# A graph network kernel on one core: order of waits in the packed attention stage, lag of twelve steps, eighteen staged chunks

## The reference, cut to what matters

```python
h = relu(layernorm(x))
x_l = h @ W_l + b_l;  x_r = h @ W_r + b_r           # 4 heads of 32
m = leaky_relu(x_l[s] + x_r[d], 0.2)                # s, d: edges and self loops
e = einsum('ehc,hc->eh', m, att)
alpha = exp(e - segment_max(e)[d]) / segment_sum(...)[d]
x = x + segment_sum(alpha * x_l[s], d) + bias
h = relu(layernorm(x))
msg = (h @ W_in2f)[src] * (ssp(f_ij @ Wf1 + bf1) @ Wf2 + bf2) * rcut
x = x + ssp(segment_sum(msg, dst) @ Wo1 + bo1) @ Wo2 + bo2
```

## Time and profile before

| what | value |
|---|---|
| median of 3 runs | 3136.14 us (3135.15 to 3142.57) |
| the profiled execution, its own time | 3137.6 us |
| its span, first to last instruction | 3135.7 us |
| mean granted clock of TensorE | 0.916 |
| busy: PE, DVE, ACT, POOL | 78%, 72%, 61%, 60% of the span |
| stage D, about 0 to 475 us | DMA engines 89% busy |
| stage A, about 475 to 1555 us | DMA engines 49% busy |
| stage B, about 1555 to 2760 us | DMA engines 61% busy |
| stage F, about 2760 to 3136 us | DMA engines 94% busy |

### The profile page before, as it was taken

One profiled execution on the slowest core, in us unless ns is written; L12 is line 12 of the kernel. 1 busy time (PEld: TensorE's weight loads), 2 busy tenths in 40 slices (PEclk: granted clock), 3 DMA queues, 4 the chain that ended last, 5 costly groups with the idle time before them and its releaser, 6 DMA issues.

```text
span 3135.7 us, 59629 instructions
## 1 busy us (share of the span) xinstructions
PE 2438.1 (78%) x16506; PEld 1688.5 (54%) x16506; DVE 2269.0 (72%) x6293; ACT 1924.9 (61%) x4383; POOL 1884.0 (60%) x1646
## 2 busy tenths in 40 slices
PE   5988897887888888888677777776777777578887
PEld 4666663344444444444455555555555555467776
DVE  6777775676777777676587777777877777557666
ACT  5888886555555555554165555555555555378887
POOL 2677774366766666672168888888878888700000
PEclk8999999999999899898598999999988988889999
DMA  7999983355545555554355666666566565589998
GB/s 215 296 322 315 288 275 127 119 168 154 163 153 168 171 178 180 149 170 139 108 117 111 120 117 113 118 114 121 113 117 115 116 121 110 136 311 424 426 426 334
DMA packets 389182, 590.96 MB, mean 188 GB/s; under 512 B 148024, under 2 KB 225196, under 8 KB 363923
## 3 DMA queue, kind: packets, MB, share of 16 engines
q1 hardware_dynamic: 291106, 478.16, 46.6%
q0 software_dynamic: 97968, 111.60, 18.7%
HBM read 352.81 MB, written 245.42 MB: 191 GB/s over the span
## 4 chain that ended last, share of the span: by engine, by line
DMA 22%; DVE 22%; issue 16%; POOL 12%; PE 12%; ACT 10%; SPq 6%; DVEq 0%; POOLq 0%; ACTq 0%
POOL sum_dram L737 7%; DMA out<-d_x 7%; DMA d_x<-in_x 4%; POOL x_dram L725 4%; DMA b_end<-ends 3%; ACT a_ns L1296 3%; DMA sum_dram<-b_sum,b_at 2%; DVE stat_e_six L958 2%; DVE a_o L1076 2%; PE bank L1530 2%; DVE a_pv L1070 2%; DVE a_gate L1068 2%; DVE stat_e_six L960 2%; DMA x_dram<-b_xo,sidx 2%; DVE stat_d_six L882 2%
## 5 line engine op out<-in xcount | busy, mean ns | idle before, releaser
L737 POOL DMA_INDIRECT sum_dram<-b_sum,b_at x392 | 636.8, 1624 | 146.7 <-issue 112.8
L651 POOL DMA_INDIRECT a_xs<-in_x,index x328 | 334.4, 1020 | 112.0 <-issue 103.7
L658 POOL DMA_INDIRECT a_xd<-in_x,index x328 | 333.0, 1015 | 100.0 <-issue 94.2
L725 POOL DMA_INDIRECT x_dram<-b_xo,sidx x294 | 314.7, 1070 | 105.9 <-issue 91.6
L1669 PE MATMUL bank<-b_rows,b_same 128*128 128x128 bf16 x4704 | 303.6, 229 | 0.6 <-ACT b_sum L1437 0.6
L1669 PEld LDWEIGHTS bank<-b_rows,b_same 128*128 128x128 bf16 x4704 | 288.7, 103 | 0.6 <-issue 0.6
L1277 ACT ACTIVATE d_n<-d_x,stat_d_shift,stat_d_rstd 128x128 f32<-128x128 f32 x686 | 283.5, 486 | 0.2 <-DVE stat_d_shift L773 0.2
L667 POOL DMA_INDIRECT x_dram<-a_xo,index x98 | 101.0, 1030 | 298.8 <-DVE a_xo L1091 280.2
L1702 PE MATMUL bank<-wo,f_ssp_out 128*128 128x128 f32 x1568 | 230.5, 294 | 62.1 <-DVE f_ssp_out L1223 60.5
L767 ACT ACTIVATE stat_e_log<-stat_e_var 128x4 f32<-128x4 f32 (+1 forms) x147 | 30.5, 208 | 370.3 <-DVE stat_e_var L763 370.3
L1702 PEld LDWEIGHTS bank<-wo,f_ssp_out 128*128 128x128 f32 x1568 | 206.3, 205 | 78.9 <-DVE f_ssp_out L1223 73.2
(11 more groups left out here) (234 smaller groups left out, 6220.9 us busy)
## 6 DMA issues: line engine op xcount, KB each, us to landing
d_x<-in_x SPq DMA_DIRECT2D x196, 256.0 KB
x_dram<-d_x SPq DMA_DIRECT2D x196, 256.0 KB
out<-d_x SPq DMA_DIRECT2D x49, 1024.0 KB, 10.1
sum_dram<-zero SPq DMA_DIRECT2D x48, 1024.0 KB
d_x<-x_dram SPq DMA_DIRECT2D x45, 1024.0 KB, 14.0
d_n<-sum_dram SPq DMA_DIRECT2D x25, 1024.0 KB, 11.9
a_beta<-beta_dram SPq DMA_DIRECT2D x392, 64.0 KB
x_end_dram<-a_xo SPq DMA_DIRECT2D x98, 256.0 KB, 2.6
```

Of the source, the lines that this page charges most:

```text
L651: pool.indirect_dma_start(a_xs[t % DEPTH][:, j * F:(j + 1) * F], None, x, column(t, j)).then_inc(gathered[t % GSEM], 16)
L658: pool.indirect_dma_start(a_xd[t % DEPTH][:, j * F:(j + 1) * F], None, x, column(t, TILES + j)).then_inc(gathered[t % GSEM], 16)
L725: pool.indirect_dma_start(x1_dram, bass.IndirectOffsetOnAxis(ap=sidx[s][:, j:j + 1], axis=0), b_xo[s][:, j * F:(j + 1) * F], None, bounds_ ...
L737: pool.indirect_dma_start(sum_dram, bass.IndirectOffsetOnAxis(ap=b_at[s][:, j:j + 1], axis=0), b_sum[s][:, j * F:(j + 1) * F], None, compu ...
```

## The change

The constants: LAG 12 for 11, STAGED 18 for 16, FIRST 18 for 20, so that the staging goes through six free ring slots instead of four. a_hd has LAG + 1 buffers, so one more. p_q goes away: run_max writes the difference over p_score, and the p_score copy of the next pack no longer waits for it.

On ACT inverse_deviation moves from the end of the odd step to the even step behind it, between the a_xs copy and norms_dst. exp of p_dif moves from the end of phase 1 to behind a_hd in phase 2; the log of p_den from behind a_hd to behind the a_xs copy; p_dec goes behind a_hd of phase 3, and the other three activations on the score differences behind the a_xs copy of phase 3; the log and exp of p_run go behind a_hd of phase 4. On DVE shifts moves ahead of a_xo; tail_sums, carry_max, carry_in, run_max and run_den stand right behind the scan a_o; carry_den goes behind a_dif of phase 2 and shares behind a_dif of phase 4.

```diff
-LAG = 11
+LAG = 12
...
-STAGED = 16
-FIRST = 20
+STAGED = 18
+FIRST = 18
...
-                dve.tensor_tensor(p_q[:, :], p_score[:, :], p_run[:, 0:C], ALU.subtract).then_inc(rows_dve, 1)
+                dve.tensor_tensor(p_score[:, :], p_score[:, :], p_run[:, 0:C], ALU.subtract).then_inc(rows_dve, 1)
...
                 if packed and phase == 2:
-                    carry_in(b)
-                if packed and phase == 3:
-                    run_den(b)
+                    carry_den(b)
+                if packed and phase == 4:
+                    shares(b)
                 if front:
...
+                if packed and phase == 0:
+                    tail_sums(b)
                 if packed and phase == 1:
                     carry_max(b)
                 if packed and phase == 2:
+                    carry_in(b)
                     run_max(b)
+                if packed and phase == 3:
+                    run_den(b)
                 if t + LEAD < NC:
                     sums_a(t + LEAD)
-                if packed and phase == 3:
-                    shares(b)
+                if t % 2 == 0 and t + 4 <= NC:
+                    pair = (t + 2) // 2
+                    shifts(dve, stat_e[pair % 2], 4 * TILES, rstd, shift, pair + 1)
                 if back:
...
-                    if b >= 1:
-                        act.wait_ge(rows_dve, by_dve(b - 1, "q"))
...
+                if t % 2 == 0 and t >= 2 and t + 4 <= NC:
+                    pair = (t + 2) // 2
+                    inverse_deviation(act, stat_e[pair % 2], 4 * TILES, var, log_var, rstd, pair + 1)
                 if ahead:
                     norms_dst(t + 1)
-                if t % 2 and t + LEAD < NC:
-                    pair = (t + LEAD) // 2
-                    inverse_deviation(act, stat_e[pair % 2], 4 * TILES, var, log_var, rstd, pair + 1)
```

More of the change, by code:

```diff
@@ L55 @@
 BY_DVE = {"max": 3, "sum": 4, "own": 6, "dif": 9, "den": 11, "q": 17, "dec": 18, "scan": 19, "beta": 20}
-BY_ACT = {"score": 1, "tail": 2, "log": 3, "ratio": 4, "lse": 5, "abs": 6, "down": 7, "decayed": 8, "up": 9, "den_log": 10, "rec": 11}
-STAGED = 16
-FIRST = 20
+BY_ACT = {"score": 1, "tail": 2, "log": 3, "ratio": 4, "lse": 5, "down": 6, "abs": 7, "decayed": 8, "up": 9, "den_log": 10, "rec": 11}
+STAGED = 18
+FIRST = 18
 SPARE = DEPTH - FIRST
@@ L196, in gnn @@
         p_tail = sb("p_tail", [PR, C + 1])
-        p_q = sb("p_q", [PR, C])
         p_dec = sb("p_dec", [PR, C])
@@ L1094, in step_a @@
                     statistics(dve, stat_e[pair % 2], 4 * TILES, six, sumdif, sq, var, pair, pair + 1)
[L1095 to L1101, removed]
             for t in range(LEAD):
@@ L1333, in step_a @@
                 if packed and phase == 2:
-                    act.wait_ge(rows_dve, by_dve(b, "den"))
-                    act.activation(p_den[:, 0:PACK], p_den[:, 0:PACK], ACT.Ln).then_inc(rows_act, 1)
+                    act.wait_ge(rows_dve, by_dve(b, "dif"))
+                    act.activation(p_exp[:, 0:PACK], p_dif[:, 0:PACK], ACT.Exp)
+                    act.activation(p_exp[:, 8:8 + PACK], p_dif[:, 8:8 + PACK], ACT.Exp).then_inc(rows_act, 1)
+                if packed and phase == 3:
+                    act.wait_ge(rows_dve, by_dve(b, "q"))
+                    act.activation(p_dec[:, :], p_score[:, :], ACT.Exp, scale=-1.0).then_inc(rows_act, 1)
+                if packed and phase == 4:
+                    act.wait_ge(rows_dve, by_dve(b, "scan"))
+                    act.activation(p_run[:, 0:C], p_run[:, 0:C], ACT.Ln, bias=1.0).then_inc(rows_act, 1)
+                    act.wait_ge(rows_act, by_act(b, "den_log"))
+                    act.activation(p_run[:, 0:C], p_run[:, 0:C], ACT.Exp, scale=-1.0).then_inc(rows_act, 1)
                 if ahead:
@@ L1347, in step_a @@
                     act.activation(p_tail[:, :], p_tail[:, :], ACT.Exp, bias=p_col[:, 1:2]).then_inc(rows_act, 1)
+                if packed and phase == 2:
+                    act.wait_ge(rows_dve, by_dve(b, "den"))
+                    act.activation(p_den[:, 0:PACK], p_den[:, 0:PACK], ACT.Ln).then_inc(rows_act, 1)
                 if packed and phase == 3:
-                    act.wait_ge(rows_dve, by_dve(b, "scan"))
-                    act.activation(p_run[:, 0:C], p_run[:, 0:C], ACT.Ln, bias=1.0).then_inc(rows_act, 1)
@@ L1351, in step_a @@
-                    act.wait_ge(rows_act, by_act(b, "den_log"))
-                    act.activation(p_run[:, 0:C], p_run[:, 0:C], ACT.Exp, scale=-1.0).then_inc(rows_act, 1)
+                    act.activation(p_tail[:, 0:C], p_score[:, :], ACT.Abs).then_inc(rows_act, 1)
+                    act.wait_ge(rows_act, by_act(b, "abs"))
+                    act.activation(p_tail[:, 0:C], p_tail[:, 0:C], ACT.Exp, scale=-1.0).then_inc(rows_act, 1)
+                    act.activation(p_up[:, :], p_score[:, :], ACT.Exp).then_inc(rows_act, 1)
```

## The result

The changed kernel takes 3018.09 us in the median of three runs (3014.57 to 3025.44), against 3136.14: 0.9622 of the time before, with a 95% interval of 0.9587 to 0.9657, 118 us less. The forecast was 3048 with a range of 3022 to 3090. The profiled execution took 3014.57 us.

What follows compares the result with a forecast made beforehand. A cycle of waits between ACT and VectorE, with no engine full, bounds the kernel. 85 x (9.42 - 10.43) = -86, front -11, back +5, staging +3 sum to -89 us: 3048 against 3136, range 3022 to 3090.

Steps and rivals of the forecast that it cites:

- The cycle: Packed attention stage: ACT waits 229.0 us for VectorE's stat_e_var ahead of a_hd; VectorE waits back 48.4 us for a_hd.
- Rival (E): VectorE's chain set the pace all along; carry_in and run_den behind the scan add 2.7 us a pack: 3184, chance 0.04.
- The count of a step from a_u to a_u: On VectorE without waits: odd step 8.74 us, even step floor 8.28, 119.1 us for seven of each.
- rival (D): New ACT waits behind a_hd in phases 2 to 4 uncovered, or loads still late: about 3100, chance 0.06.
- Term (1) and (2): ACT's inverse deviation behind the a_xs copy, VectorE's shifts ahead of a_xo: costed at nothing, or about 0.4 us per even step.
- Step (4): Slow PE clock after long stalls: one such step kept in 14, +1.8 us, making 9.42 a step; none makes 9.29.
- the 2.67 us from a_dif to a_u: VectorE's time from a_dif's start to a_u's start, 1.98 of it idle for PE's product and ACT's copy; this stays.
- Step (5): a_gate's load stall of 26.5 us: gone, with shares moved and twelve steps of lag; already outside the 9.42.
- Step (6): The lag: one more front-only and back-only step, one full step fewer; front -11 us, back +5.
- Step (7): Staging: two more staged chunks store 2 x 512 KB, up to 3.4 us, taken as 3; gathers on POOL hidden.
- Rival (B): POOL becomes the bound, its need 8.9 us a step rising as gathers lengthen; at 9.75 a step 3077 us, chance 0.13.
- (F): VectorE holds GpSimd at nearly each gather, all at 1557 ns: 12.3 us a step, time 3293, chance 0.01.

## Why the prediction was right, and where it was not

**The cycle** (ACT's wait for the variance ahead of a_hd, VectorE's wait back): right. Moving those two activations and the shift alone gave 65 us; putting them back cost 85. Rival (E), that ACT's wait was only a shadow of VectorE's chain, would have had them give nothing.

**The count of a step from a_u to a_u**: right in form. Even steps without packed work are 8.28 as predicted. A small operation behind the scan costs an odd step nearly its whole length and one ahead of a_u costs nothing, which is what the 5.9 us a pack rested on. tail_sums (9.15 - 8.57), carry_max (0.69) and run_den (1.89) came as priced. Phase 2 stands above its term in the list above (11.10 for 10.67, 11.96 for 11.34), but over the twelve packs it goes from 10.56 to 11.10 and from 11.21 to 12.09, and the shortest are below their terms. All of that spread lies between the next a_dif and a_u, and it is PE's clock: v_mm of the step behind, in two packs, and the clock at the second,

```profile
816.03 1.13 PE L1586 MATMUL bank<-a_dif,wl 128*128 128x512 f32 x2 [2.67 <-DVE a_dif L1048]
...
944.21 2.01 PE L1586 MATMUL bank<-a_dif,wl 128*128 128x512 f32 x2 [2.66 <-DVE a_dif L1048]
...
945.00:946.00 1.00, 1.00 (x2) 0.23 (x1) 0.00 (x0) 0.00 (x0) 0.77 (x1) 0.50 0.33 84
```

PE has waited equally long for an a_dif that run_max holds back; in one pack v_mm then takes 1.13 us, in the other 2.01 at a granted 0.50. ACT's wait for run_max before p_dec looks like rival (D) and is not: it is 2.24 to 2.26 us in all twelve, and a_ns behind it is done before v_mm ends in each.

**Term (1) and (2), activations behind the a_xs copy and the shift**: right, cost nothing: a_dif has no idle time ahead of it in the full steps, but for 0.44 us in the first.

**The failed step is the size of a full step**, 9.42 forecast and 9.16 measured, 22 us over 85 steps. It has two parts. Step (4) kept one slow-clock step in 14, 1.8 us each, 11 us in all. In the trace v_mm is lengthened in seven of the twelve phase-3 steps, by 0.2 to 0.9 us each and 3.1 us in all; in the second trace of the changed kernel it is nine and 6.7 us. I priced the slow steps as a remainder of the old mean clock instead of asking what would still make PE wait long: the load stall no longer does, run_max in phase 2 does, for 2.0 to 2.7 us.

And the 2.67 us from a_dif to a_u were read in a step whose a_dif had itself waited for a_hd. PE's self_mm waited for the same a_hd, here over the stretch of the earlier trace rows:

```profile
PE bank L1587 <- ACT a_hd L1324: 87.5, 42, 5.2
```

It stood right ahead of v_mm and pushed it back, which started 0.98 us after a_dif; now self_mm is over in time, v_mm starts 0.74 after a_dif, and the chain takes 2.54. This is 0.13 to 0.17 us in the 11 of 14 steps that VectorE sets, about 10 us. The 4 us that are left I did not take apart.

**Step (5), the load stall gone**: right, and only with twelve steps of lag. **Step (6)**: front -11.7 for -11, right. The back was to cost +5 and gave -1.3: the tail of the old kernel held a load stall of 4.3 us too, now 1.2, which the count of one more back step at 5 to 6 us left out; the other 3 us stay open. **Step (7)**: no cost for the stores, where I took 3 from a range of 0 to 3.4. The start of the stage moved by 0.1 us.

**Rival (B)**, POOL as the bound, did not come true in the changed kernel: two chunks less to gather (STAGED 20) make it no faster. But it was closer than the prediction had it, by its own mechanism. POOL's need was put at 8.9 us a step and is 9.1, as its items take 1.39 us with the gap and not 1.35, the scatters above all. And I treated the staging as a cost only, where with 16 staged chunks the lack of it costs 20 us. A chunk whose rows come late stops VectorE at once.

**A sum that was off.** (D) has 3 us a pack and 3 for the rest, which is 45 us in 14 packs and not 50; it moves that rival's time by 5 us and nothing else.

**The range.** Its low end was the sum's lower case, 3034, less 12. That case held two of the too dear terms (2.67, and the tail). Slow clock, tail and stores together were 8 + 6 + 3 us, all to the same side.

## What to carry to other kernels

Look for the instruction that everybody needs first in a step, and see what waits ahead of it on its own engine: a wait for the last thing of the step before belongs behind it. Around such a cycle, put small work under a wait that is there anyway, rather than behind the operation that sets the pace; and when a step gets shorter, recheck what had just enough time: here a load that needed one more step of lag, and GpSimd's gathers, which two constants had to relieve. Of a duration that is to be kept, take it from a step in which its own engine had not been waiting.

## What the runs showed of the hardware

In this kernel PE's slow stretches follow its waits, and most went away with them: the granted clock of the stretch rose from 0.93 to 0.98 without any change in PE's instructions, and by the intervals counted above, less the 3.1 us that are left, some 24 of the 108 us of the full steps came from there. Equal waits need not end alike: behind 2.7 us, v_mm took 1.13 us in one pack and 2.01 in another.

GpSimd's gathers bear a busier VectorE well, its scatters less so. The changed kernel's gathers, 570 to 1354 us, as group and as durations, and the durations of all scatters of the stage, before and now:

```profile
L650 POOL DMA_INDIRECT a_xs<-in_x,index x224 | 240.6, 1074 | 68.3 <-issue 61.6 <-DVE a_xo L1096 6.7
...
L650 POOL DMA_INDIRECT a_xs<-in_x,index x224: 942/947/1608, 587.1 to 1315.2; - x112
...
L667 POOL DMA_INDIRECT x_dram<-a_xo,index x98: 977/1011/1282, 587.1 to 1552.1; - x98
...
L666 POOL DMA_INDIRECT x_dram<-a_xo,index x98: 976/1118/2227, 585.7 to 1431.3; - x98
```

VectorE went from 71% to 81% busy and the mean gather from 1048 to 1074 ns, the median stayed at 947 for 948. The median scatter went from 1011 to 1118 ns. What lengthens the scatters is not shown: VectorE is busier, and so are the DMA engines, at 0.59 for 0.52.

The lock that the Trainium skill describes (SBUF — State Buffer, section "SBUF: two separate sides") holds for a VectorE operation with two SBUF inputs only against a GpSimd operation that reads SBUF, a condition that (B) and (F) left out. No run here shows whether a gather is one. If it were, the median gather should have grown with VectorE's share, and it did not; that decides against (F).
